# A seventeenth lane in the score products: the distance penalty becomes one more summand of the reduction

## The reference

```python
rel = |arange(K) - K // 2|
scores = stack([einsum('blhd,blhd->blh', q, k_pad[:, w:w + L]) for w in range(K)], axis=-1) * SCALE
soft_mask = sigmoid((width[..., None] - rel) * sharp[..., None])
attn = softmax(scores - (1.0 - soft_mask) * MASK_PENALTY, axis=-1)
out = sum(attn[..., w][..., None] * v_pad[:, w:w + L] for w in range(K))
x = layernorm(x + silu(out @ Wout))
```

## Time and profile before

| what | value |
|---|---|
| median of the runs | 1171.63 us |
| profiled execution | 1173.19 us, span 1170.8 us |
| mean granted TensorE clock | 0.929 |
| busy: PE, DVE, POOL, ACT | 952.9, 821.6, 711.4, 461.5 us |
| window loop, 150 to 440 us: DVE, POOL, PE, ACT busy of 290.0 | 287.34, 275.55, 266.48, 123.79 us |

### The profile page before, as it was taken

How to read it: one execution, slowest core, us unless ns; L and a number is a source line. 1 busy time by engine, 2 the same in 40 slices (tenths; PEclk the granted TensorE clock), 3 DMA queues, 4 the chain that set the end, 5 groups by cost and what they waited for, 6 DMA issues and landing times.

```text
span 1170.8 us, 24977 instructions
## 1 busy us (share of the span) xinstructions
PE 952.9 (81%) x8069; PEld 768.7 (66%) x8070; DVE 821.6 (70%) x1260; ACT 461.5 (39%) x1068; POOL 711.4 (61%) x461
## 2 busy tenths in 40 slices
PE   7994089998998989858888349999999999999940
PEld 4542088888988988746666237777777777777730
DVE  4899999999999998238888774444444444444435
ACT  3676224434444544425656322222222222222215
POOL 3575599999999999300001055666666766666522
PEclk9998589999999999979999669999999999999985
DMA  3272011121122112476684401222222222222236
GB/s 103 72 120 50 30 41 62 52 67 51 61 67 67 59 53 67 163 260 220 215 276 170 166 24 39 47 40 45 45 45 45 41 46 43 45 45 41 33 84 226
DMA packets 69914, 100.23 MB, mean 86 GB/s; under 512 B 9248, under 2 KB 51680, under 8 KB 68928
## 3 DMA queue, kind: packets, MB, share of 16 engines
q1 hardware_dynamic: 52816, 76.86, 21.2%
q0 software_dynamic: 15904, 18.66, 10.0%
q10 hardware_dynamic: 1152, 4.19, 0.9%
HBM read 73.83 MB, written 26.25 MB: 85 GB/s over the span
## 4 chain that ended last, share of the span: by engine, by line
PE 44%; DVE 28%; issue 15%; DMA 5%; ACT 3%; POOL 3%; DVEq 1%; SPq 0%; ACTq 0%; POOLq 0%
PE psum L760 16%; DVE mid L1408 11%; PE psum L768 10%; PE psum L770 5%; PE psum L619 3%; DVE psum L1415 2%; DMA sum_dram<-arena,mid 2%; PE psum L599 2%; PE psum L662 2%; PE psum L752 2%; DVE arena L1562 1%; ACT arena L1098 1%; PE psum L711 1%; PE psum L602 1%; DMA out<-arena 1%
## 5 line engine op out<-in xcount | busy, mean ns | idle before, releaser
L619 PE MATMUL psum<-consts,mid 128*128 128x128 f32 x2176 | 256.5, 280 | 58.0 <-POOL mid L1171 58.0
L619 PEld LDWEIGHTS psum<-consts,mid 128*128 128x128 f32 x2176 | 253.4, 196 | 64.9 <-issue 48.2
L760 PE MATMUL psum<-arena 128*128 128x128 f16 x3408 | 286.9, 220 | 4.1 <-issue 3.8
L760 PEld LDWEIGHTS psum<-arena 128*128 x3408 | 239.8, 98 | 74.7 <-issue 8.8
L1171 POOL TENSOR_TENSOR mid<-arena 128x2304 f32<-128x2304 f32 (+1 forms) x62 | 251.1, 4072 | 9.9 <-POOL arena L1162 6.7
L768 PE MATMUL psum<-arena 128*128 x568 | 215.1, 380 | 4.9 <-DVE arena L1719 1.2
L1249 POOL DMA_INDIRECT sum_dram<-arena,mid x71 | 141.3, 1991 | 43.4 <-issue 20.5
L1728 DVE SCALAR_TENSOR_TENSOR arena<-psum,arena 128x256 f32<-128x256 f32 x71 | 34.3, 484 | 186.0 <-ACT arena L1068 131.6
L770 PE MATMUL psum<-arena 128*128 x568 | 154.8, 273 | 0.0
L1068 ACT ACTIVATE arena<-psum,arena 128x256 f32<-128x256 f32 x71 | 33.6, 473 | 296.3 <-PE psum L770 296.3
L1408 DVE TENSOR_TENSOR mid<-psum,arena 128x4352 f32<-128x4352 f32 x32 | 149.8, 4683 | 0.6 <-issue 0.4
(11 more groups left out here) (196 smaller groups left out, 1436.0 us busy)
## 6 DMA issues: line engine op xcount, KB each, us to landing
arena<-w_t SPq DMA_DIRECT2D x64, 256.0 KB, 2.8
arena<-w_t SPq DMA_DIRECT2D x16, 1024.0 KB, 10.8
arena<-x SPq DMA_DIRECT2D x32, 128.0 KB, 2.1
arena<-x_dram SPq DMA_DIRECT2D x8, 512.0 KB, 5.2
arena<-ctx_t SPq DMA_DIRECT2D x8, 512.0 KB, 6.1
arena<-ctx SPq DMA_DIRECT2D x8, 512.0 KB, 6.7
x_dram<-mid SPq DMA_DIRECT2D x8, 512.0 KB, 3.3
arena<-sum_dram SPq DMA_DIRECT2D x8, 512.0 KB, 4.9
```

Of the source, the lines that this page charges most:

```text
L619: last = nc.tensor.matmul(psum[:, u, c * P:(c + 1) * P], products[half][:, w, c * P:(c + 1) * P], ident, start=(a + w == 0 and c == 0), st ...
L760: last = nc.tensor.matmul(dst, block_of(w, e, 0, c * F + j * P, P), x[:, u, c * P:(c + 1) * P], start=(k == 0 and c == 0), stop=(k == 2 an ...
```

## The change

`qk_prod` becomes 17 rows by 16 heads by 17 numbers (`LANES = D + 1`): 16 products and, as the seventeenth, the penalty. ACT writes that lane for step t+1 right behind its exponential of step t, in two instructions (`lay_penalties`), after the reduction of step t has read the old one. DVE's multiply leaves the lane free; its reduction sums 17 numbers and writes straight to `score`; the two additions of the penalty go. The reduction now waits for the lanes, and for the same `prob_made` that the additions waited for. In step 0 the reduction moves behind `last_gates`, and ACT lays the lane of step 0 before the second half of the gates. `mid` grows by 272 numbers; `ones_pp` becomes a column that is read as a broadcast, and the unused `reach` constants go, to make room.

```diff
-        qk_prod = mid[:, 0:K * E]
+        qk_prod = carve(mid, 0, K, H, LANES)
...
+            def lay_penalties(t, gate_at):
+                if past(t, 1):
+                    act.wait_ge(qk_summed, t)
+                gates = row(gate, t + gate_at).rearrange("p a h r -> p r (a h)")
+                lane = qk_prod[:, :, :, D]
+                nc.scalar.activation(lane[:, R:, :], gates, ACT.Copy, scale=-PENALTY / SCALE).then_inc(penalties_laid, 1)
+                nc.scalar.activation(lane[:, R - 1::-1, :], gates[:, 1:, :], ACT.Copy,
+                                     scale=-PENALTY / SCALE).then_inc(penalties_laid, 1)
...
                 nc.scalar.activation(score[:, u, :], score[:, u, :], ACT.Exp, scale=SCALE).then_inc(exp_done, 1)
+                if not isinstance(t, int) or t < CHUNK - 1:
+                    lay_penalties(t + 1, gate_at)
                 if more:
                     copy_queries(t + 2, u)
...
             win_sigmoids(1)
             head_roots(GROUPS - 1)
+            act.wait_ge(gate_done, 1)
+            lay_penalties(0, GROUP)
             gates(1)
...
+            def sum_products(t, u):
+                dve.wait_ge(qk_multiplied, t + 1)
+                dve.wait_ge(penalties_laid, 2 * t + 2)
+                if past(t, 2):
+                    dve.wait_ge(prob_made, t - 1)
+                nc.vector.tensor_reduce(score[:, u, :].rearrange("p (h w) -> p w h", w=K), qk_prod, op=ALU.add,
+                                        axis=AX.X).then_inc(qk_summed, 1)
...
-                nc.vector.tensor_tensor(qk_prod[:, :].rearrange("p (w c) -> p w c", c=E), queries,
-                                        k_all[:, bass.ds(t, K), :], ALU.mult).then_inc(qk_multiplied, 1)
+                nc.vector.tensor_tensor(qk_prod[:, :, :, 0:D], queries.rearrange("p w (h d) -> p w h d", d=D),
+                                        k_all[:, bass.ds(t, K), :].rearrange("p w (h d) -> p w h d", d=D),
+                                        ALU.mult).then_inc(qk_multiplied, 1)
...
-                dve.wait_ge(qk_multiplied, t + 1)
-                nc.vector.tensor_reduce(raw.rearrange("p (h w) -> p w h", w=K),
-                                        qk_prod[:, :].rearrange("p (w h d) -> p w h d", h=H, d=D), op=ALU.add, axis=AX.X).then_inc(qk_summed, 1)
+                if not (isinstance(t, int) and t == 0):
+                    sum_products(t, u)
                 if past(t, 1):
                     invert(t - 1, 1 - u)
                 if isinstance(t, int) and t == 0:
                     last_gates()
-                    dve.wait_ge(gate_done, 1)
+                    sum_products(0, 0)
...
                 dve.wait_ge(qk_summed, t + 1)
-                if past(t, 2):
-                    dve.wait_ge(prob_made, t - 1)
-                nc.vector.scalar_tensor_tensor(by_head[:, :, R:], gates, -PENALTY / SCALE, raw_by_head[:, :, R:],
-                                               ALU.mult, ALU.add).then_inc(penalised, 1)
-                nc.vector.scalar_tensor_tensor(by_head[:, :, R - 1::-1], gates[:, :, 1:], -PENALTY / SCALE,
-                                               raw_by_head[:, :, R - 1::-1], ALU.mult, ALU.add).then_inc(penalised, 1)
-                dve.wait_ge(penalised, 2 * t + 2)
                 nc.vector.tensor_reduce(peak[:, u, :], score[:, u, :].rearrange("p (h w) -> p h w", w=K), op=ALU.max,
                                         axis=AX.X).then_inc(peak_found, 1)
```

More of the change, by code:

```diff
@@ L39 @@
 W0 = (K + 1) // 2
+LANES = D + 1
+QK = K * H * LANES
 ORDER = tuple(range(CHUNK - GROUP, CHUNK)) + tuple(range(CHUNK - GROUP))
@@ L46 @@
 MASKED = 1e10
-LOW = 10856
+LOW = 10824
 N_EXP, TOP, F = 8, 2, 1024
@@ L61 @@
 AT_IDENT = 0
-AT_REACH = AT_IDENT + P
-AT_MASK = AT_REACH + K
+AT_MASK = AT_IDENT + P
 AT_BELOW = AT_MASK + P
@@ L78, in host_consts @@
         i == j,
-        wide(np.abs(np.arange(K) - R)),
         np.where(j > i, -MASKED, 0.0),
@@ L148, in decoder_layer @@
         big = arena[:, LOW:]
-        mid = sb("mid", [P, 2 * K * E])
+        mid = sb("mid", [P, QK + K * E])
         low_used = {}
@@ L173, in decoder_layer @@
         ident = consts[:, AT_IDENT:AT_IDENT + P]
-        reach = consts[:, AT_REACH:AT_REACH + K]
-        ones_pp = sb("ones_pp", [P, P])
+        ones_col = sb("ones_col", [P, 1])
+        ones_pp = ones_col[:, :].to_broadcast([P, P])
         minus_half = sb("minus_half", [P, 2 * H])
@@ L251, in decoder_layer @@
         w_exp = carve(mid, scale_at + 8, 2).bitcast(I32)
-        assert scale_at + 10 <= 2 * K * E
+        assert scale_at + 10 <= QK + K * E
         gate_col = next_low("experts", 4, 1)
@@ L274, in decoder_layer @@
         v_all = carve(big, (CHUNK + ROWS) * E, ROWS, E)
-        qk_prod = mid[:, 0:K * E]
-        av_prod = [carve(mid, K * E, W0, E), carve(mid, (K + W0) * E, K - W0, E)]
+        qk_prod = carve(mid, 0, K, H, LANES)
+        av_prod = [carve(mid, QK, W0, E), carve(mid, QK + W0 * E, K - W0, E)]
         av_last = [carve(mid, 0, W0, E), carve(mid, W0 * E, K - W0, E)]
         x_step = carve(mid, 0, 2, X_QUAD, C, P)
[L280 to L283, removed]
+        act_qk = carve(mid, QK, 2, 2 * E)
+        cen_qk = carve(mid, QK + 4 * E, 2, 2 * E)
+        sq_qk = carve(mid, QK + 8 * E, 2, 2 * E)
+        head_r = carve(mid, QK + 12 * E, GROUP, 2 * H)
         gate = next_low("window", CHUNK, H, R + 1)
@@ L390, in decoder_layer @@
         qk_summed = sem("qk_summed")
-        penalised = sem("penalised")
+        penalties_laid = sem("penalties_laid")
         q_beside = sem("q_beside")
@@ L646, in _ @@
             pe.wait_ge(w_summed, 1)
-            nc.tensor.matmul(psum[:, 0, 0:2], ones_pp[:, :], w_sum[:, :], start=True, stop=True).then_inc(w_total, 1)
+            nc.tensor.matmul(psum[:, 0, 0:2], ones_pp, w_sum[:, :], start=True, stop=True).then_inc(w_total, 1)
             def transpose_x1(u, c):
@@ L728, in _ @@
                              picked.rearrange("p t n -> p (t n)"), start=True, stop=True)
-            nc.tensor.matmul(psum[:, 1, 0:TILES * N_EXP], ones_pp[:, :],
+            nc.tensor.matmul(psum[:, 1, 0:TILES * N_EXP], ones_pp,
                              picked.rearrange("p t n -> p (t n)"), start=True, stop=True).then_inc(counted, 1)
@@ L885, in copy_queries, with window @@
                 nc.scalar.activation(q_psum[:, u:u + 1, :], row(q_all, t), ACT.Copy).then_inc(q_beside, 1)
-            def window(t, u, i, more=True):
+            def lay_penalties(t, gate_at):
[6 more added lines that the diff above has]
+                                     scale=-PENALTY / SCALE).then_inc(penalties_laid, 1)
+            def window(t, u, i, gate_at, more=True):
                 act.wait_ge(score_ready, t + 1)
                 nc.scalar.activation(score[:, u, :], score[:, u, :], ACT.Exp, scale=SCALE).then_inc(exp_done, 1)
+                if not isinstance(t, int) or t < CHUNK - 1:
+                    lay_penalties(t + 1, gate_at)
                 if more:
@@ L945, in _ @@
             head_roots(GROUPS - 1)
+            act.wait_ge(gate_done, 1)
+            lay_penalties(0, GROUP)
             gates(1)
-            steps(act, LAG, window, LAG)
-            steps(act, CHUNK - 2, window, LAG, LAG)
+            act.wait_ge(gate_done, 2)
+            turn = CHUNK - GROUP
+            steps(act, LAG, lambda t, u, i: window(t, u, i, GROUP), LAG)
+            steps(act, turn - 2, lambda t, u, i: window(t, u, i, GROUP), LAG, LAG)
+            window(turn - 2, 0, turn // 2 - 1, GROUP)
+            window(turn - 1, 1, turn // 2 - 1, GROUP - CHUNK)
+            steps(act, CHUNK - 2, lambda t, u, i: window(t, u, i, GROUP - CHUNK), turn, turn)
             for t in range(CHUNK - 2, CHUNK):
-                window(t, t % 2, t // 2, more=False)
+                window(t, t % 2, t // 2, GROUP - CHUNK, more=False)
             for t in range(CHUNK - LAG, PARTS[2][1]):
@@ L1113, in _ @@
             nc.gpsimd.memset(v_all[:, R + CHUNK:ROWS, :], 0.0).then_inc(halo_zeroed, 1)
-            nc.gpsimd.memset(ones_pp[:, :], 1.0).then_inc(fills_made, 1)
+            nc.gpsimd.memset(ones_col[:, :], 1.0).then_inc(fills_made, 1)
             nc.gpsimd.memset(minus_half[:, :], -0.5).then_inc(fills_made, 1)
@@ L1402, in last_gates, with window @@
                     gate_args(1, r)
-            def window(t, u, i, gate_at):
+            def sum_products(t, u):
[5 more added lines that the diff above has]
+                                        axis=AX.X).then_inc(qk_summed, 1)
+            def window(t, u, i):
                 dve.wait_ge(q_beside, t + 1)
                 queries = q_psum[:, u:u + 1, :].to_broadcast([P, K, E])
-                nc.vector.tensor_tensor(qk_prod[:, :].rearrange("p (w c) -> p w c", c=E), queries,
-                                        k_all[:, bass.ds(t, K), :], ALU.mult).then_inc(qk_multiplied, 1)
+                nc.vector.tensor_tensor(qk_prod[:, :, :, 0:D], queries.rearrange("p w (h d) -> p w h d", d=D),
```

(6 more changed lines are left out.)

3 lines of the change are left out of this document (removed).

## The result

The changed kernel takes 1165.77 us (median of five runs, 1164.58 to 1166.83), the kernel before 1171.17 beside it (five runs, 1169.87 to 1171.71): ratio 0.9949, interval 0.9937 to 0.9962, so 5.4 us less where 4.2 were forecast, and 0.03 us below the range's lower end of 1165.8. The forecast of 1167.4 was counted from 1171.63; of the 1.6 us between it and 1165.77, 1.2 are the larger gain and 0.4 come from the kernel before, whose median was 1171.17 this time. In a second measurement (e1) the ratio is 0.9943, interval 0.9926 to 0.9960. The direction was right, and so was the main reason for it; the size was too small. The profiled execution took 1166.83 us, its span 1164.9.

A forecast was written before the change was run, and what follows sets the result against it. DVE was taken to lead the window loop with POOL some 4% behind; POOL's 4.8 us of waits less 0.1 left and 0.6 for step 0 gave 4.2 us, 1171.6 to 1167.4 us, range 1165.8 to 1170.9.

The forecast's parts named there:

- POOL takes over as the bound: Window loop: eight steps cost DVE 83.9 us against POOL's 85.2, so POOL never catches up after its first `norm_part`.
- the ceiling: Window loop, 150 to 440 us: POOL's waits for DVE's peak, 4.8 us in 13 steps, cap the gain.
- The 41.47 us: POOL's time for four loop steps taken as free of waits for DVE, 262.38 to 303.85, or 10.37 each.
- the 0.1 us of waits: POOL's waits for DVE assumed to remain up to step 11, where the two engines were judged level.
- DVE's saving: Each loop step: two additions go (0.53 us), the reduction grows by 0.28, net 0.25 us less.
- the lanes: ACT's two added instructions per step, 0.31 and 0.30 us: 0.43 to 0.5 us more, bounds 0.43 and 0.62, hidden in idle time.
- step 0: First loop step: moving the reduction behind `last_gates` makes POOL's first subtraction 0.6 us later.
- the multiply: DVE's multiply with gaps after every 16 numbers: no added cost assumed, bounds nothing and 0.19 us; 4.68 us expected.
- the reduction: DVE's reduction over 17 numbers: 272 more numbers cost 0.28 us, 4.97 us in all.
- Rival 1: Window loop: all of DVE's saving arrives, 7.2 us, giving 1164.4 us; chance 0.06.
- Rival 2: Gaps cost DVE's multiply: one payment per run 1170.6 us, chance 0.12; two payments 1176.0, slower case, chance 0.09.
- Rival 3: ACT's lanes come late, 2 us instead of 0.52, delaying steps behind each `norm_part`: 1169.8 us; chance 0.11.

The follow-up runs named there:

- e1: The changed kernel measured again with no edit: 1165.88 us, ratio 0.9943 against the kernel before.
- e3: On the changed kernel, POOL's silu product moved one step later, into its wait for its own probabilities: 1162.22 us, ratio 0.9904.
- e4: On the kernel before, POOL's silu product moved one step later, into its wait for its own probabilities: 1172.22 us, ratio 0.9998.
- e6: On the changed kernel, the reduction sums only 16 of the 17 numbers, leaving the penalty out of the scores: 1164.68 us, ratio 0.9927.
- e10: e3 with the reduction summing only 16 of the 17 numbers, leaving the penalty out of the scores: 1159.20 us, ratio 0.9874.
- e5: On the kernel before, ACT's two lane instructions added, writing to unread spare space, with the new memory layout: 1173.32 us, ratio 1.0004.
- e2: On the changed kernel, DVE's reduction of step 0 put back under the square root: 1166.06 us, ratio 0.9943.
- e9: e2 and e3 together on the changed kernel: 1161.07 us, ratio 0.9897.

## Why the prediction was right, and where it was too small

*Right: POOL takes over as the bound.* "After the first `norm_part` POOL never catches up, so nearly all of its 4.8 us of waits go": they went entirely, and e3, e4, e6 and e10 show the pair from both sides. A cut on DVE is worth nothing in the loop with POOL at 10.30 and 2.9 us with POOL at 9.97; a cut on POOL is worth nothing with DVE at 10.67 and 3.7 us with DVE at 10.29.

*Failed: the ceiling.* "All its waits for DVE's peak are 4.8 us ... That row is the ceiling of the change." It wasn't. The stretch from step 4 to 28 shrank by 5.6 us, 0.8 more than that row, and the sum had 4.7. Step by step, a listed wait of 0.42 or 0.32 stood for a step 0.46 or 0.36 longer than in the changed kernel; over the 13 steps this is 0.4 us. The other 0.4 us lie in steps without a listed wait. The 41.47 us that I took for four free steps of POOL were not free. Step 16 was 0.12 us long: the earlier trace rows has no wait at 303.85, but that subtraction started 0.1 us after DVE's peak had ended, and the view doesn't list so short a wait. POOL's timeline and then DVE's, kernel before:

```profile
303.03 0.74 POOL L1176 TENSOR_TENSOR arena<-arena 128x256 f32<-128x256 f32 x1
```

```profile
303.33 0.44 DVE L1436 TENSOR_REDUCE arena<-arena 128x16 f32<-128x272 f32 x1
```

Step 14 was 0.15 us long, and step 22 0.19, because PE's slow sums held POOL up. POOL's timeline in step 13, kernel before:

```profile
274.39 8.09 POOL L1171 TENSOR_TENSOR mid<-arena 128x2304 f32<-128x2304 f32 x2 [0.47 <-PE psum L619]
```

In e5, where the sums are quick, these two steps take 10.29 and 10.31. POOL's free step is 10.30, and the kernel before has it already in the steps 13 and 15 (10.29 and 10.31). A better working would have been 21 steps of 10.30 and three of 12.6 with their norm parts: 254.1 us from step 4 to 28, against 253.81 measured. Of the 0.9 us that the forecast lacked in this stretch the ceiling is 0.8, and the 0.1 us of waits that I had left up to step 11 is the rest.

*Left out: the clock.* Part of the larger gain comes by a way that the prediction has no term for. The lanes' work on ACT splits PE's pause, and the sums behind it stay quick (e5). On the kernel before this is worth nothing, but with DVE faster nothing would hide the 0.15 and 0.19 us. No run has the change with the slow sums, so that this is worth about 0.3 us is my estimate from the steps 14 and 22, and not shown.

*Mis-sized: DVE's saving*, 0.38 us a step from step 8 on (e3) where the sum had 0.25. L1431 had started 0.25 us behind the start of the reciprocal; the peak starts 0.16 behind it, and is itself 0.40 us and not 0.44. I had let the peak take L1431's place together with that gap. L1431's address changes with the step and comes from a register in the loop, the peak's is fixed. In the steps that are written out L1431 too starts 0.16 behind the reciprocal, and there the saving is 0.26. Behind POOL the mistake cost the forecast no more than the 0.1 us of waits named above. DVE's timeline in a step written out, kernel before:

```profile
194.83 0.24 DVE L1446 RECIPROCAL arena<-arena 128x16 f32<-128x16 f32 x1
194.99 0.27 DVE L1431 SCALAR_TENSOR_TENSOR arena<-arena,psum 128x144 f32<-128x144 f32 x1
```

*Mis-sized: the lanes*, 0.68 us of ACT's step for 0.43, over the upper bound of 0.62. It fitted into ACT's waits, as argued; e5 puts its price at nothing measurable.

*Right:* step 0 (+0.68 for +0.6, and e2 and e9 trace it to the move of the reduction), the multiply (4.68) and the reduction (4.97).

*Not settled:* the stretch behind the loop. The loop from step 4 on and step 0 give 5.0 us together, the medians 5.4 and 6.3. From step 28 to the first scores of cross attention it is 74.4 us in the mean of the two executions before and 73.5 in those after, but the two before differ by 1.4. So up to a microsecond of the 5.4 to 6.3 us could come from there or be scatter.

*The rivals.* Rival 1 asked for POOL to give way, which it doesn't on its own; e3 had to move work to let it. Rival 2, the gaps, is excluded by 4.68. The rule of the Trainium skill named in the prediction ("SBUF — State Buffer", section "Door 1: The DMA port swizzle", on 16-byte cachelines) doesn't show in the multiply, whose runs of 16 leave the lines; the trace agrees with it where single numbers are far apart: L893 takes 0.46 us for 144 numbers, and the contiguous L899 0.42 for 272. Rival 3 set in nowhere: even 0.65 us later the lanes leave POOL's rhythm as it is.

## What to carry to other kernels

When two engines run within a few per cent of each other, take the follower's period from steps in which it certainly waits for nobody, then multiply; the sum of its listed waits is too low. The time that a cut on the leader gives is the difference between the two, and the next cut belongs on the other engine: 0.3 us that POOL spent waiting for its own result were worth 3.7 us, but only after DVE's cut. An instruction moved out from under a latency lays the latency bare, here 1.0 us at the first subtraction; one more move took it back there (e2, e9), and in e9 it was kept to the end of the loop.

## What the runs showed of the hardware

TensorE's granted clock fell behind the pauses of the loop. PE's timeline behind the third norm part, kernel before, then changed:

```profile
436.10 1.13 PE L628 MATMUL psum<-arena 128*128 128x256 f32 x4 [0.57 <-ACT arena L869]
...
440.25 9.49 PE L619 MATMUL psum<-consts,mid 128*128 128x128 f32 x68 [2.16 <-POOL mid L1171]
```

```profile
433.50 1.13 PE L628 MATMUL psum<-arena 128*128 128x256 f32 x4 [1.25 <-ACT arena L869]
...
436.99 7.86 PE L619 MATMUL psum<-consts,mid 128*128 128x128 f32 x68 [1.49 <-POOL mid L1191]
```

The granted clock of the 5 us from 440 was 0.66, in the changed kernel from 436.7 on 1.00 (the number behind POOL's busy time, kernel before and then changed):

```profile
440.00:445.00 5.00, 4.75 (x28) 4.75 (x29) 4.96 (x6) 1.38 (x5) 5.00 (x4) 0.66 0.28 105
```

```profile
436.70:441.70 5.00, 4.71 (x42) 4.71 (x43) 5.00 (x4) 1.91 (x7) 5.00 (x4) 1.00 0.41 130
```

A clock of 0.66 over the stretch means that a part of it ran at 1.2 GHz and the rest at 2.4. Before the fall PE had idled 0.57 and then 2.16 us; where it idled 1.25 and 1.49 the clock stayed. Judged by the time of the sums, 9.4 to 9.5 us or 7.86, that held in all six such places of the two executions before (fell), and in the three each of changed, e1 and e5 (stayed). In e4 the sums stayed at 7.86 us twice, with idles of 1.97 and 1.85 before them, and took 9.49 once with 1.84, so the length of that idle alone doesn't decide. In e3 and e9, with idles of 0.55 to 0.62 and then 1.67 to 1.82, they stayed at 7.86 in all six places. What decides between these is open. In the prediction I had not expected that work added on ACT would keep TensorE fast, nor that sums 1.63 us quicker at three places would be worth nothing on the kernel before.
